# The tail of a vision tower kernel on one core: expert sums on TensorE, throttled node gathers, five batches, a shorter gate function and a short last scan

## What is computed

```python
h = (x_flat @ W_gat).reshape(M, HEADS, NUM_EXPERTS)
e = leaky_relu(a_src[src] + a_dst[dst], 0.2)
e_max = segment_max(e, dst);  ee = exp(e - e_max[dst])
denom = segment_sum(ee, dst)
agg = segment_sum(h[src] * (ee / denom[dst])[:, :, None], dst) + b_gat
scores = layernorm(agg, ln_gamma, ln_beta).reshape(M, HEADS, NUM_EXPERTS).mean(1)
topk_s, topk_i = top_k(scores, 2);  w = softmax(topk_s)
for ei in range(NUM_EXPERTS):
    g = where(topk_i == ei, w, 0.0).sum(-1)
    hh = gelu(x @ W1[ei] + b1[ei])
    out = out + g[..., None] * (hh @ W2[ei] + b2[ei])
return h_in + out
```

## Time and profile before

| | |
|---|---|
| median of 3 runs | 4125.78 us (4123.27 to 4126.69) |
| the profiled execution | 4124.24 us, its span 4122.1 us |
| busy | PE 1795.9 us (44%), DVE 2288.7 (56%), ACT 1160.8 (28%), POOL 2534.4 (61%) |
| chain that ended last | POOL 52%, issue 17%, PE 4%, DVE 3% |
| last edge gather issued | 3844.89 us |
| last scan on DVE | 3847.39 to 3870.79 us |
| first node gather issued | 3885.26 us |
| node and gate part of the four batches begins | 3936.34, 3994.19, 4047.11, 4091.70 us |
| last store issued, end of the span | 4119.53, 4122.1 us |

### The profile page before, as it was taken

One profiled execution on the slowest core, in us unless ns is written; L12 is line 12 of the kernel. 1 busy time (PEld: TensorE's weight loads), 2 busy tenths in 40 slices (PEclk: granted clock), 3 DMA queues, 4 the chain that ended last, 5 costly groups with the idle time before them and its releaser, 6 DMA issues.

```text
span 4122.1 us, 27660 instructions
## 1 busy us (share of the span) xinstructions
PE 1795.9 (44%) x7311; PEld 767.6 (19%) x7311; DVE 2288.7 (56%) x3931; ACT 1160.8 (28%) x1699; POOL 2534.4 (61%) x2473
## 2 busy tenths in 40 slices
PE   2651114869995976759204672553743000000000
PEld 1211112323332322323101231221311000000000
DVE  7898887868886886868445453353020120220268
ACT  1320002536663644535103452342532000000000
POOL 1000002747777777777777777777777777777473
PEclk9875556989997988879557896886866555555555
DMA  5220001444554544434252332232332111111134
GB/s 118 42 48 0 0 0 37 85 67 87 89 97 77 96 85 74 85 58 77 43 43 59 68 85 44 62 69 45 110 82 78 27 27 10 27 24 25 22 86 146
DMA packets 651776, 247.81 MB, mean 60 GB/s; under 512 B 552244, under 2 KB 632420, under 8 KB 649188
## 3 DMA queue, kind: packets, MB, share of 16 engines
q1 hardware_dynamic: 573700, 216.76, 22.8%
q0 software_dynamic: 77920, 29.29, 7.8%
HBM read 152.68 MB, written 91.71 MB: 59 GB/s over the span
## 4 chain that ended last, share of the span: by engine, by line
POOL 52%; issue 17%; PE 4%; DVE 3%; DMA 2%; DVEq 1%; SPq 0%; ACT 0%; POOLq 0%; ACTq 0%
POOL ring L744 49%; POOL ring L758 2%; DMA ring<-table,src_i 2%; PE ps L841 1%; PE ps L831 1%; DVEq L1708 1%; PE ps L856 1%; POOL adst_d L721 0%; DVE arena L1709 0%; PE ps L882 0%; PE ps L890 0%; DVE arena L1711 0%; PE ps L833 0%; PE ps L904 0%; PE ps L898 0%
## 5 line engine op out<-in xcount | busy, mean ns | idle before, releaser
L744 POOL DMA_INDIRECT ring<-table,src_i x2048 | 2089.5, 1020 | 654.4 <-issue 645.2
L1514 DVE TENSOR_TENSOR_SCAN ad<-ns,cad,raw 128x128 f32<-128x128 f32 x64 | 25.9, 465 | 1092.9 <-DMA ring<-table,src_i 997.0
L710 POOL DMA_INDIRECT ring<-keys_d,place x128 | 144.9, 1132 | 712.0 <-DVEq L1189 670.0
L945 PE MATMUL ps<-arena 64*128 64x512 f32 x800 | 223.1, 680 | 534.4 <-ACT arena L1127 278.3
L1047 ACT ACTIVATE arena<-ps,tb 128x448 f32<-128x448 f32 x504 | 296.0, 632 | 267.3 <-PE ps L841 148.1
L1052 ACT ACTIVATE ex<-ex 128x1024 f32<-128x1024 f32 x16 | 16.9, 1056 | 1181.9 <-DVE ex L1530 1181.9
L1558 DVE TENSOR_TENSOR arena<-arena 128x448 f32<-128x448 f32 x504 | 292.1, 617 | 92.7 <-ACT arena L1047 91.2
L992 PE MATMUL ps<-ident,ends 128*20 128x128 f32 x6 | 1.5, 418 | 744.9 <-DVEq L1734 744.9
L841 PE MATMUL ps<-arena,w 64*128 64x448 f32 x896 | 243.2, 621 | 146.4 <-ACT arena L1041 126.3
L1127 ACT ACTIVATE arena<-ps,arena 128x1024 f32<-128x1024 f32 x200 | 213.4, 1116 | 127.5 <-PE ps L945 127.3
L856 PE MATMUL ps<-arena,w 128*64 128x448 f32 x896 | 199.2, 565 | 41.6 <-issue 41.6
(11 more groups left out here) (332 smaller groups left out, 3442.3 us busy)
## 6 DMA issues: line engine op xcount, KB each, us to landing
arena<-in_x SPq DMA_DIRECT2D x304, 110.0 KB
ring<-table,src_i POOLq DMA_INDIRECT x2048
partial<-res SPq DMA_DIRECT2D x16, 1536.0 KB, 6.0
arena<-in_x SPq DMA_DIRECT2D x160, 140.0 KB
outputs_d<-arena SPq DMA_DIRECT2D x32, 512.0 KB
arena<-outputs_d SPq DMA_DIRECT2D x32, 512.0 KB, 4.6
arena<-xnT SPq DMA_DIRECT2D x100, 128.0 KB, 3.2
arena<-h_tok SPq DMA_DIRECT2D x50, 256.0 KB, 3.1
```

The source lines that it names most:

```text
L744: g.indirect_dma_start(out=ring[k % 2][:, j - k * SC, :], out_offset=None, in_=table[0:GRAPH_NODES, :], in_offset=off(ap=src_i[:, j:j + 1] ...
L945: m = mm(hid[ee % 2][:, z * NT:(z + 1) * NT], fw1[lower_upper(z), ee, :], xf[q][lower_upper(z), :], start=True, stop=True)
```

## The change

Five edits, all of which act after the front:

1. **Scan sizes.** The 2048 columns are cut into 15 chunks of 128, one of 96 and one of 32, 17 in place of 16. `own` and `nrow` change rings, and so the load of `own` is issued after the scan of the 96.
2. **Node batches** of 24, 32, 32, 24, 16 columns, five in place of four; 6, 8, 8, 6 and 4 halves.
3. **Node gathers in groups of 4,** at most two groups under way, as for the edges (`node_group`).
4. **Gate function.** The mean over heads is taken before the multiplication by the inverse root, so the latter, and the addition of beta (its sum over heads, `betsum`, is computed once), work on 4 values per row instead of 16. One reduction takes the place of three additions, the multiplication by gamma stands ahead of the wait for ACT, and two scalar operations are fused into others.
5. **Combine part of the graph rows.** DVE only multiplies by the weights (into one of three buffers `yb`). PE adds the four experts and the residual in PSUM with five accumulating matmuls by the identity matrix, 256 columns each, and ACT copies the sum to `yo`. SP stores a pair when ACT has copied it, one pair later in its stream than before, and the load of `hr` is issued behind that store. DVE may be three halves ahead of PE.

```diff
-SCHUNKS = COLS // SC
+SIZES = [SC] * (COLS // SC - 1) + [96, 32]
+SCHUNKS = len(SIZES)
+FROM = [sum(SIZES[:k]) for k in range(SCHUNKS)]
...
-NODE_BATCHES = [(0, 40), (40, 80), (80, 112), (112, 128)]
-NB = 40
+NODE_BATCHES = [(0, 24), (24, 56), (56, 88), (88, 112), (112, 128)]
+NB = 32
...
+        last_ring = (SCHUNKS - 1) % 2
+        own = ring[1 - last_ring]
...
+            def node_group(n, j):
+
+                half = j // GROUP % 2
+                if j % GROUP == 0:
+                    of = n if j - 2 * GROUP >= NODE_BATCHES[n][0] else n - 1
+                    if of >= 0:
+                        pool.wait_ge(nrows[of % 2][half], node_count(of, half, j - GROUP))
+                return nrows[n % 2][half]
...
-                store_out(OUT_PAIRS + m)
-                if m + 2 < GRAPH_PAIRS:
-                    load_h(OUT_PAIRS + m + 2)
+                if m:
+                    store_out(OUT_PAIRS + m - 1)
+                    if m + 1 < GRAPH_PAIRS:
+                        load_h(OUT_PAIRS + m + 1)
+            store_out(PAIRS - 1)
...
+            for hidx in range(2 * GRAPH_PAIRS):
+                k, z = OUT_PAIRS + hidx // 2, hidx % 2
+                o = bank(1 + hidx % 4)[:, 0:FF * CH]
+                pe.wait_ge(S["halves_gated"], hidx + 1)
+                if z == 0:
+                    pe.wait_ge(ff[k % 2], 32 * (OUT_PAIRS // 2) + 16 * ((k - OUT_PAIRS) // 2 + 1))
+                wait(pe, S["halves_out"], hidx - 3)
+                for ee in range(EXPERTS):
+                    mm(o, ident[:, :], yb[hidx % 3][:, :, ee, :], start=ee == 0, stop=False)
+                mm(o, ident[:, :], hr[k % 2][:, z, :, :], start=False, stop=True).then_inc(S["halves_summed"], 1)
...
                 gate_fn(len(GATE_BATCHES) + n, j1 - j0, g1[:, j0:j1, :])
+                for hidx in range(j0 // FF, j1 // FF):
+                    k, z = OUT_PAIRS + hidx // 2, hidx % 2
+                    act.wait_ge(S["halves_summed"], hidx + 1)
+                    if z == 0:
+                        act.wait_ge(ost[k % 2], 16 * (k // 2))
+                    a(yo[k % 2][:, z, :, :].rearrange("p j c -> p (j c)"), bank(1 + hidx % 4)[:, 0:FF * CH], ACT.Copy)\
+                        .then_inc(S["halves_out"], 1)
...
-                    lambda: v.tensor_scalar(R, R, 1.0 / HE, None, ALU.mult),
-                    lambda: v.tensor_tensor(T, T, R.unsqueeze(2).broadcast_to([P, K, HE]), ALU.subtract),
+                    lambda: v.scalar_tensor_tensor(out=T, in0=R.unsqueeze(2).broadcast_to([P, K, HE]), scalar=-1.0 / HE,
+                                                   in1=T, op0=ALU.mult, op1=ALU.add),
...
+                v.tensor_tensor(T, T, bc(gam), ALU.mult)
+                v.tensor_copy(A3, base[:, :].unsqueeze(1).broadcast_to([P, K, EXPERTS]))
+                v.drain()
+                v.tensor_reduce(A2, T.rearrange("p k (h e) -> p k e h", h=HEADS), AX.X, ALU.add)
+                v.drain()
                 dve.wait_ge(S["g_std"], n + 1)
-                seq(lambda: v.tensor_tensor(T, T, R.unsqueeze(2).broadcast_to([P, K, HE]), ALU.mult),
-                    lambda: v.tensor_tensor(T, T, bc(gam), ALU.mult),
-                    lambda: v.tensor_tensor(T, T, bc(bet), ALU.add),
-                    lambda: v.tensor_tensor(A2, T[:, :, 0:4], T[:, :, 4:8], ALU.add),
-                    lambda: v.tensor_tensor(A2, A2, T[:, :, 8:12], ALU.add),
-                    lambda: v.tensor_tensor(A2, A2, T[:, :, 12:16], ALU.add),
-                    lambda: v.tensor_copy(A3, base[:, :].unsqueeze(1).broadcast_to([P, K, EXPERTS])))
+                seq(lambda: v.tensor_tensor(A2, A2, R.unsqueeze(2).broadcast_to([P, K, EXPERTS]), ALU.mult),
+                    lambda: v.tensor_tensor(A2, A2, betsum[:, :].unsqueeze(1).broadcast_to([P, K, EXPERTS]), ALU.add))
...
-                    combine(OUT_PAIRS + hidx // 2, hidx % 2, yback[hidx % 4],
-                            g1[:, hidx * FF:(hidx + 1) * FF, :].rearrange("p j e -> p (j e)"), S["yb_read"])
+                    wait(dve, S["halves_summed"], hidx - 2)
...
+                    v.tensor_tensor(yb[hidx % 3].rearrange("p j e c -> p (j e) c"),
+                                    yback[hidx % 4].rearrange("p (n c) -> p n c", c=CH),
+                                    gates_z.unsqueeze(2).broadcast_to([P, FF * EXPERTS, CH]), ALU.mult)
+                    v.drain()
+                    v.nop().then_inc(S["halves_gated"], 1)
+                    v.nop().then_inc(S["yb_read"], 1)
```

More of the change, by code:

```diff
@@ L354, in build, with node_count @@
         off = bass.IndirectOffsetOnAxis
+        def node_count(n, half, upto):
+            return 16 * sum(j // GROUP % 2 == half for a, b in NODE_BATCHES[n % 2:n + 1:2] for j in range(a, min(b, upto)))
         def x_loads(s):
@@ L1789, in wide @@
                     return t.unsqueeze(3).broadcast_to([P, K, HEADS, EXPERTS])
[L1791 removed]
+                for half in range(2):
+                    dve.wait_ge(nrows[n % 2][half], node_count(n, half, k1))
                 seq(lambda: v.tensor_tensor(new, nr[:, :, 0:HEADS], self_e[:, ks_n, :], ALU.max),
```

119 lines of the change are left out of this document (66 added, 53 removed).

## The result

| | before | after |
|---|---|---|
| median of the runs, us | 4126.23 (4123.27 to 4130.65, 6 runs) | 4093.68 (4092.41 to 4096.81, 6 runs) |
| ratio, 95% interval | | 0.9921 [0.9908, 0.9933] |
| profiled execution, own time (span), us | 4124.24 (4122.1) | 4096.81 (4095.1) |
| last edge gather issued | 3844.89 | 3845.32 |
| from there to the first node gather (T = 0) | 40.37 | 25.45 |

The change saves 32.5 us by the medians, 27.4 by the two profiled executions. The forecast was a gain of 24.0 and 4101 us. The profiled execution of after happens to be the longest of its six, 3.1 us above their median. The comparison by stretches depends less on that: the three stretches in the last rows of the table add up to the span. The change was meant for the second and third.

The account below looks back on a forecast made before the run. The kernel was taken as one long queue of GpSimd gathers plus a tail. First node gather 11.7 us earlier and 12.3 us less after it gave 24.0 us, 4124.24 to 4100.2, stated as 4101 us; range 4089 to 4117.

Parts of the forecast that it names:

- short last scan: Between last edge gather and first node gather: 13.3 us saved plus 1.2, less 2.8, so 11.7 us earlier; bounds 8.5 and 14.5.
- the term taken off: At the edge gathers: 2.5 us for scanning 96 columns beside them and 0.3 for the extra store, 2.8 us lost.
- The gate function's large calls: Three large calls before the expert stage: hidden behind the edge gathers, so 0 gained.
- The third stretch: From the first node gather (T) to the end of the span: T + 224.5 instead of 236.8; bounds 219.5 and 232.
- 88 gathers landed, batch 2 starts: Batch 2 needs 88 node gathers: 108.8 us, 7 for work beside them, landed 2.4 later, T + 118.2.
- eight halves until ScalarE is free: Combine part of eight halves, paced by TensorE at 2.3 us per half and by hr loads: 24.6 us.
- TensorE's sums are no better than VectorE's: Combine parts of eight, six, four halves: 24.6, 19.3, 12.9 us with TensorE's sums, against 23.6, 17.7, 11.8 on VectorE before.
- Rival (a): Node gathers slowed or held back, 1.9 us per step beside combine and 1.5 beside the rest: T + 234, 4111 us; chance 0.14.
- over 1.6: Sign against the forecast: gathers stepping over 1.6 us beside the combine part, where 1.45 was taken.
- Rival (b): Combine parts: TensorE's granted clock stays at 0.50, a half costs 4.3 us, T + 261, 4137 us, slower; chance 0.08.
- Rival (c): Better: loads land sooner, scans shrink more, fewer gathers collide; both lower bounds, 4093 us; chance 0.10.
- Rival (d): No gain: first node gather not earlier, as own's load and the stores delay edge gathers, and gathers slow: 4121 us; chance 0.06.

Follow-up runs that it names:

- control: The changed kernel itself run again, nothing altered, beside the last three follow-up kernels: 4095.02 us, ratio 0.9918 to the kernel before.
- Doubled work: The changed kernel with TensorE's sum of each half done twice into the same bank (ten matmuls): 5707.69 us, ratio 1.0109 to the kernel before, on the slow chip.
- half an undo: The changed kernel with the expert sums back on VectorE but SyncE's order of stores and hr loads left as changed: 4115.73 us, ratio 0.9972 to before.
- three pieces: The changed kernel with the next exponential before the last two copies, four hr buffers and last scans of 80, 32, 16: 4080.67 us, ratio 0.9884 to before.
- three sets: Twelve follow-up kernels in three groups, each group on one chip beside the kernel before, which took 5650.68 us in the second.

## Why the prediction was right, step by step

**The short last scan was mis-sized, by 4 us.** Its gross gain was right: 13.3 + 1.2 = 14.5 us forecast, 40.37 - 25.45 = 14.9 measured (13.9 against the changed kernel without it). The scan itself became 23.45 - 10.19 = 13.3 us shorter, as forecast. What failed is the term taken off, 2.8 us for the edge gathers. Its pieces were 2.5 us for the scan of 96 columns beside them, 0.3 for own and the extra store, and a wait of 2.02 us that would move along. The scan cost 1.9 us. The wait shrank to 1.04 us, so 1.0 came back. And a pause that I had not looked for is gone; before, 14 gathers ahead of the last one, it stands here:

```profile
3824.54 0.94 POOL L744 DMA_INDIRECT ring<-table,src_i  x1 [0.30 <-issue]
3827.41 0.94 POOL L744 DMA_INDIRECT ring<-table,src_i  x1 [1.93 <-issue]
```

It stands there in the kernel without the short last scan too (2.02 us) and in neither the changed kernel nor its control; what it is stays open. Together 1.9 - 1.0 - 1.6 = -0.7 us, which is the 165.8 against 166.5. So the term is 14.9 + 0.7 = 15.6 us where 11.7 was forecast, above its own upper bound of 14.5. T was forecast at 3873.6 and is 3870.77, which is just inside those bounds, but only because gather 1919, from which the last 128 steps count, came 1.1 us later than before.

**The gate function's large calls were put at 0, "hidden behind the edge gathers".** They aren't hidden: the gathers beside them are what bounds there, and they became 3 to 4 us shorter in all, as the experiment with the old gate function shows. With 15.6 and the 12.5 us of the third stretch that makes some 31.6 us, and 32.5 were measured by the medians. The forecast of 24.0 was short by these two terms, 3.9 and 3 to 4 us.

**The third stretch came out to 0.2 us** (T + 224.5 forecast, 224.33 measured; 223.94 in the control), and its parts one by one:

| | forecast | measured in after |
|---|---|---|
| 88 gathers landed, batch 2 starts | T + 118.2 | T + 119.6 |
| node and gate part, 32 columns | 18.8 | 18.9 |
| eight halves until ScalarE is free | 24.6 | 24.0 |
| batch 3: rest of its node and gate part, six halves | 15.3 + 19.3 | 15.3 + 18.6 |
| batch 4: rest, four halves | 12.8 + 12.9 | 12.8 + 12.5 |
| last store | 2.6 | 2.7 |

The errors of +1.4 and -0.6, -0.7, -0.4 cancel, so the 0.2 us is in part luck. The small ones fit a copy of 0.38 us where 0.47 was taken and a half of 2.16 us where 2.3 stood. The forecast's claim behind this term, that TensorE's sums are no better than VectorE's, is now shown to about 1 us: T + 225.05 with VectorE's. The gate function gives 5.9 to 7.3 of the 12.5 us (7.2 in the sum). The rest, 4 to 6 us with TensorE's 1 us taken off, is put down to batches of 24, 32, 32, 24 and 16 instead of 40, 40, 32 and 16. That is a remainder: no kernel ran with the old batches, so it isn't shown.

**Rival (a), slowed gathers,** was in part what happened. Between gathers 73 and 83, beside the products of batch 1, a step took 1.66 us on average in after and 1.55 in the control; 1.45 was taken, and "over 1.6" was named as a sign against the forecast. Over all three combine parts that still have gathers it was 1.68 in after (28 steps) and 1.53 in the control (32), so by this sign the forecast was wrong in one of two executions of the same kernel. Over T to batch 2 this cost 1.4 us in after and nothing in the control (117.56), because only 13 of its 88 gathers begin beside a product. A gather that does so is held by up to 1.0 us, as the rows of the last section show. The Trainium skill (SBUF — State Buffer, Who interferes with whom) has such a rule: a VectorE instruction with two inputs in SBUF contends with a GpSimd one that reads SBUF. The trace agrees for gathers that begin inside a product; the prediction had left out the condition on the GpSimd instruction, and no row here shows a product held by a gather.

**Rival (b), a low clock,** fell: the granted clock was 0.50 when TensorE began a combine part and 1.00 in nearly all the rest of it (0.50 from 3964 to 3969 and 1.00 from there to 3988 in batch 1), so that only the first half costs more, 3.64 to 4.43 us. The gap of 1.97 us before 3973.64 didn't bring it down. The Trainium skill (TensorE: Matmul & The Clock Gate, HAM oscillation) tells of falls in waits for transfers; no gap inside a combine part here did that. The 262 cycles that the Trainium skill (TensorE: Matmul & The Clock Gate, Back-to-back issue gap) gives for 256 columns would by estimate have made a half 0.55 us; the rows give 2.16, four times as much for this type, and they decide. Doubled work, the same 4.3 us per half that a low clock would have cost, took batch 2 to the end from about 105 to 151 us, 46 us more, though on the slow chip. The rival had put 36.5 us (T + 261 instead of T + 224.5) on such a half, which was no exaggeration.

**Rival (c), the lower bounds,** came nearest in the total, 4093 against 4093.68, but by luck. Of what it named nothing is seen: the last scan shrank by the 13.3 us of the forecast, and gathers beside products cost more than forecast, not less; that loads landed sooner isn't shown. The 7 us between 4101 and the median are about the size of the two terms above.

**Rival (d), no gain,** fell with the 15.6 us of the last scan. The total alone would not have told the forecast from (c), since 4093.68 lies 7.3 us under the one and 0.7 above the other; the stretches do.

## What to carry to other kernels

Freeing the engine that binds gives nothing if a third engine passes the result on: look where in its queue the next stage's first instruction stands. Here one exponential placed two copies earlier was worth 10 us, about as much as the whole shorter gate function (5.9 to 7.3 us in the tail and 3 to 4 ahead of it), while the move of the sums to TensorE was worth about 1.

When one part of a change is undone, undo its order of transfers too; half an undo measured a wait that neither kernel has. And where executions differ by several us upstream, compare stretches from a common event, not totals; but look for every place at which an edited function is called, or an effect ahead of that event is taken for noise.

## What the runs showed that was not expected

*A gather that begins beside a product waits for its end.* Beside the products of batch 0 in after, two steps from one gather to the next take 2.23 and 2.16 us:

```profile
3926.95 1.22 DVE L1867 TENSOR_TENSOR arena<-arena 128x1024 f32<-128x1024 f32 x1 [1.00 <-PE ps L1038]
3927.07 1.92 POOL L789 DMA_INDIRECT ring<-partial,ends_i  x1 [0.30 <-issue]
3929.30 1.85 POOL L789 DMA_INDIRECT ring<-partial,ends_i  x1 [0.30 <-issue]
```

The product at 3926.95 lasts 1.22 us, and the gather that begins 0.1 us into it ends 0.8 us after it, though an undisturbed one takes 0.94. That holds without exception: all 21 node gathers of after that begin inside a product, 0.09 to 1.03 us after its start, end 0.81 to 0.83 us after its end, and in the kernel before 19 of 19 do. The products take 1.22 to 1.23 us whether a gather overlaps them or not, and a gather that began undisturbed before a product keeps its 0.94 us.

What matters is the second input from SBUF. Earlier in after, L1760 is the same multiplication, 128x1024 and 1.22 us long, with one input in PSUM; all 67 gathers that begin inside one of them take 0.94 or 0.95 us. One of the large calls of the gate function shows both cases within 3 us:

```profile
2093.43 1.64 DVE L1723 TENSOR_TENSOR arena<-arena,gam 128x1424 f32<-128x1424 f32 x1
2093.97 1.92 POOL L774 DMA_INDIRECT ring<-table,src_i  x1 [0.30 <-issue]
2095.57 2.67 DVE L1726 TENSOR_REDUCE arena<-arena 128x356 f32<-128x1424 f32 x1
2096.19 0.94 POOL L774 DMA_INDIRECT ring<-table,src_i  x1 [0.31 <-issue]
```

The multiplication with two inputs stretches its gather to 1.92 us, the reduction with one input leaves its gather at 0.94, though it is the longer of the two. A call of the old gate function has six operations of the first kind on 1424 values and three on 356 up to this place, a call of the new one four, two on 356 and this reduction. That fits the 3.5 us less that the edge gathers take beside them. The rule of the Trainium skill named above agrees with all of this in the one direction that the trace shows.

Where products come at TensorE's pace, steps of 2.15 to 2.16 us stand in row after row (8 of the 13 steps over 1.6 us with the three pieces are 2.15 or 2.16): the gathers have fallen into the pace of the products, one per product. With VectorE's sums, products 2.95 us apart, no step beside a combine part exceeds 1.69. So TensorE's sums make gathers dearer beside a combine part (1.53 to 1.70 us a step on average, by execution, against 1.47), which gives back a little of what they free.

*One chip of the three sets was over a third slower* (5650.68 us for the kernel before, 4126.38 and 4129.57 on the two others), with waits of 23 us for loads beside gathers that kept their 1.25 us. Against the 4126 us of another chip, all four kernels of that set would have looked far slower than the kernel before.

*The last edge gather moved by 6 us* between executions of six kernels alike up to there, from 3839.93 to 3846.28. Part of it is there at the first edge gather already (1081.5 to 1085.2 us), part comes between the first and the last (2758.5 to 2764.0 us). The old gate function's kernel, at 3850.82, isn't one of them: its large calls cost 3 to 4 us on the way. What moves the others stays open.
